# Four load buffers in the last stage of a convolution and mixture-of-experts kernel, and another order of its first loads

## What is computed

```python
def _branch(x, w, d):
    f = lax.conv_general_dilated(x, w, (1, 1), [(d, d), (d, d)], rhs_dilation=(d, d), ...)
    f = jax.nn.softmax(f.reshape(N, g, K, H * W), axis=2)
    out = jnp.einsum('ngrkp,ngkp->ngrp', patches, f)
...
y = lax.conv_general_dilated(cat, w_proj, (1, 1), ...) + b_proj
x = x + relu(_group_norm(y, gn_gamma, gn_beta))
t = _to_tokens(x)                      # (2 * 9216, 256)
for e in range(8):
    h = gelu(tokens @ w1[e] + b1[e], approximate=False)
    out = out + combine[:, e:e+1] * (h @ w2[e] + b2[e])    # tokens = layer norm of t
x = _from_tokens(t + out)
```

## Time and profile before

| | us |
|---|---|
| median of 3 runs | 2598.38 |
| lowest and highest of them | 2595.76, 2602.71 |
| the profiled execution, in all | 2577.68 |
| its span, from the first to the last instruction | 2575.9 |
| last stage in that span, from the first load to the end | 2342.6 to 2575.9 |
| busy in the span: PE, DVE, ACT, POOL | 1997.6, 1636.2, 1257.9, 1087.0 |

### The profile page before, as it was taken

How to read it: one execution, slowest core, us unless ns; L and a number is a source line. 1 busy time by engine, 2 the same in 40 slices (tenths; PEclk the granted TensorE clock), 3 DMA queues, 4 the chain that set the end, 5 groups by cost and what they waited for, 6 DMA issues and landing times.

```text
span 2575.9 us, 60532 instructions
## 1 busy us (share of the span) xinstructions
PE 1997.6 (78%) x20124; PEld 1892.3 (73%) x20125; DVE 1636.2 (64%) x4385; ACT 1257.9 (49%) x2705; POOL 1087.0 (42%) x1444
## 2 busy tenths in 40 slices
PE   5898999999799798787877836451999999993332
PEld 5897999999799697777777725451999999993222
DVE  4576666665677576465555546454877888885554
ACT  4575443333477454444444434341777777771111
POOL 3566223222376413444344405675555566562000
PEclk9999999999799798788887955555999999996555
DMA  5332555665433366557566486544666555555887
GB/s 136 98 99 64 168 152 140 174 170 146 122 105 93 93 191 176 164 171 211 172 202 177 141 286 204 200 162 131 193 202 195 151 155 154 153 151 195 270 303 266
DMA packets 334947, 433.65 MB, mean 168 GB/s; under 512 B 87469, under 2 KB 260141, under 8 KB 333805
## 3 DMA queue, kind: packets, MB, share of 16 engines
q1 hardware_dynamic: 260945, 294.85, 39.6%
q0 software_dynamic: 41024, 97.10, 10.8%
q10 hardware_dynamic: 32784, 39.07, 4.6%
HBM read 277.12 MB, written 159.94 MB: 170 GB/s over the span
## 4 chain that ended last, share of the span: by engine, by line
PE 47%; DMA 13%; issue 13%; DVE 7%; ACT 6%; another core or an unknown queue 4%; POOL 4%; SPq 3%; DVEq 2%; POOLq 0%; ACTq 0%
PE ps_y L418 15%; PE ps_a L418 7%; PE ps_o L1022 6%; PE ps L418 5%; PE ps_b L959 4%; DMA expert_out<-e_out,dest 4%; DMA o_y<-expert_out 3%; DMA o_acc<-res_scratch 3%; POOL taps L2174 2%; POOL expert_out L2264 2%; PE ps_r L1135 1%; PE ps_tok L856 1%; DMA e_x<-expert_in 1%; PE ps_a L900 1%
## 5 line engine op out<-in xcount | busy, mean ns | idle before, releaser
L418 PE MATMUL ps_y<-cat_hi,wp 128*128 128x288 f32 x2048 | 496.2, 317 | 13.3 <-issue 9.6
L2220 POOL DMA_DIRECT2D patches<-rows_scratch x348 | 194.8, 599 | 594.9 <-PE ps_o L1009 398.5
L2264 POOL DMA_INDIRECT expert_out<-e_out,dest x304 | 316.9, 1042 | 237.7 <-issue 121.0
L418 PEld LDWEIGHTS ps_y<-cat_hi,wp 128*128 128x128 f32 x2048 | 363.7, 199 | 19.1 <-issue 18.0
L2174 POOL TENSOR_TENSOR taps<-taps,g_rows 96x108 f32<-96x108 f32 (+3 forms) x440 | 252.4, 600 | 168.6 <-ACT g_rows L1270 164.7
L418 PE MATMUL ps_y<-cat_lo,wp 128*128 128x288 f32 x1024 | 313.6, 306 | 7.1 <-issue 7.1
L1696 DVE SCALAR_TENSOR_TENSOR cat_lo<-ps_o,cat_hi 128x288 fp32r<-128x288 f32 (+1 forms) x576 | 228.4, 421 | 134.2 <-ACT cat_hi L1349 84.4
L1343 ACT ACTIVATE bands<-ps_b 112x288 f16<-112x288 f32 (+4 forms) x256 | 105.2, 411 | 401.7 <-PE ps_b L959 324.8
L1349 ACT ACTIVATE cat_hi<-ps_o 128x288 fp32r<-128x288 f32 (+1 forms) x576 | 213.3, 384 | 136.6 <-remote 73.5
L1688 DVE SCALAR_TENSOR_TENSOR bands<-ps_b,bands 112x288 f16<-112x288 f32 (+4 forms) x256 | 116.9, 457 | 250.5 <-ACT bands L1343 216.7
L418 PE MATMUL ps<-e_hi,w_now 128*128 128x256 f32 x1216 | 242.9, 283 | 0.4 <-issue 0.4
(11 more groups left out here) (242 smaller groups left out, 4961.1 us busy)
## 6 DMA issues: line engine op xcount, KB each, us to landing
e_x<-expert_in SPq DMA_DIRECT2D x152, 260.0 KB
o_y<-expert_out SPq DMA_DIRECT2D x48, 768.0 KB, 5.7
patches<-rows_scratch SPq DMA_DIRECT2D x160, 192.0 KB
patches<-rows_scratch SPq DMA_DIRECT2D x256, 108.0 KB
patches<-rows_scratch SPq DMA_DIRECT2D x192, 112.0 KB
x_in<-in_x SPq DMA_DIRECT2D x48, 384.0 KB, 3.7
rows_scratch<-rows_st SPq DMA_DIRECT2D x48, 384.0 KB, 4.3
y_scratch<-y_acc SPq DMA_DIRECT2D x48, 384.0 KB
```

The costliest lines, as they stand in the source:

```text
L418: mm = eng.matmul(out, lhs[p], rhs[q], start=start and n == 0, stop=stop and n == 2)
L2220: pool.dma_start(patch_target(s, n), patch_source(m, s, n)).then_inc(patch_pooled[s % RING], 16)
L2264: pool.indirect_dma_start(out=ys_dram, out_offset=bass.IndirectOffsetOnAxis(ap=at, axis=0), in_=e_out[:, u, j], in_offset=None).then_inc(e ...
```

## The change

It has three parts.

1. **Last stage.** `o_y`, `o_acc` and the semaphores `o_loaded` become four (`OB = 4`); `o_sum`, `ps_t` and `o_out` stay two. The four `o_` tensors are now allocated where `w1` and `w2`, the experts' weights, lie, which are dead by then. All loops of the stage run over four groups instead of two.
2. **Start.** SyncE issues `ident`, the first two `x_in`, `wg_stage` and one bias before the barrier, with semaphores of their own; nine constants follow one by one in its iterations 3 to 11. The splits of `wg` and `wp_own` come behind the first normalisation, that of `wp` behind step 0. ScalarE's first `keep_own` waits for all three splits, since `y_acc` lies over `wp_stage`.
3. **`sel` and the codes** are issued by ScalarE, after its steps 4 and 10, instead of by SyncE in iteration 6.

```diff
+OB = 4
+        with ExitStack() as r1:
+            o_y = sbuf(r1, "o_y", [128, OB, TT, TOP, C])
+            o_acc = sbuf(r1, "o_acc", [128, OB, TT, C])
+            o_sum = sbuf(r1, "o_sum", [128, 2, TT, C])
+            o_out = sbuf(r1, "o_out", [128, 2, CC, TC])
         w1 = sbuf(ctx, "w1", [128, E, 2, CC * C], F32R)
...
-        N_CONST = 12
+        N_CONST = 9
...
+            sp.dma_start(ident[:], a["k_ident"]).then_inc(ident_in, 16)
+            for k in range(2):
+                sp.dma_start(x_in[:, k], x_dram[0, :, :, k * T:(k + 1) * T]).then_inc(x_loaded[k], 16)
+            sp.dma_start(wg_stage[:], a["w_gen"]).then_inc(first_in, 16)
+            sp.dma_start(gn_par[:, 0], a["b_proj"]).then_inc(bias_in, 16)
...
-                    if k == 6 and m == 0:
-                        sp.dma_start(sel[:], a["k_sel"]).then_inc(c_consts_in, 16)
-                        sp.dma_start(filt_t[2 * FCOL:KF], a["k_codes"]).then_inc(c_consts_in, 16)
+                    if m == 0 and 3 <= k < 3 + len(later):
+                        dst, src = later[k - 3]
+                        sp.dma_start(dst, src).then_inc(consts_in, 16)
...
             def load_outputs(t, residual):
-                for u in range(2):
+                for u in range(OB):
...
-                    wait(sp, o_summed, t * 2 + (u + 1))
+                    wait(sp, o_summed, t * OB + (u + 1))
...
-            pe.wait_ge(consts_in, 16 * N_CONST)
+            pe.wait_ge(ident_in, 16)
...
+                    if m == 0 and k == 0:
+                        pe.wait_ge(w_lo_done, 1)
                     tap_products(k, 0)
...
+                    if m == 0 and k == 0 and o == 0:
+                        act.wait_ge(bias_in, 16)
+                        act.wait_ge(w_lo_done, 3)
                     n = unit_at["own", m, k, o]
...
+                    if m == 0 and k == 0:
+                        weights_hi(2)
+                    if m == 0 and k == 4:
+                        act.dma_start(sel[:], a["k_sel"]).then_inc(c_consts_in, 16)
+                    if m == 0 and k == 10:
+                        act.dma_start(filt_t[2 * FCOL:KF], a["k_codes"]).then_inc(c_consts_in, 16)
...
-                        wait(act, o_stored[u], t * 16 + m * (16 * CPAIRS))
+                        wait(act, o_stored[u], t * (8 * OB) + (m * (16 * CPAIRS) + n // 2 * 16))
...
-                wait(dve, o_turned, t * 2 + (u + 1))
+                wait(dve, o_turned, t * OB + (n + 1))
```

More of the change, by code:

```diff
@@ L313, in build @@
                 dest = sbuf(r2, "dest", [128, 2, S // 128], I32)
-            with ExitStack() as r2:
-                o_y = sbuf(r2, "o_y", [128, 2, TT, TOP, C])
-                o_acc = sbuf(r2, "o_acc", [128, 2, TT, C])
-                o_sum = sbuf(r2, "o_sum", [128, 2, TT, C])
-                o_out = sbuf(r2, "o_out", [128, 2, CC, TC])
         with ExitStack() as r1:
@@ L840, in _ @@
                 if m:
+                    pe.wait_ge(consts_in, 16 * N_CONST)
                     group_sums(0, ps_a)
@@ L908, in turn_filters @@
                     pe.wait_ge(f_split, m * BATCHES + b + 1)
+                    if m == 0 and b == 0 and h == 0:
+                        pe.wait_ge(consts_in, 16 * N_CONST)
                     for r in range(R2 // 2):
@@ L1217, in _ @@
             enter(pe, 7 * N_ENG)
-            with pe.Fori(0, PAIRS) as t:
-                for u in range(2):
-                    wait(pe, o_summed, t * 2 + (u + 3))
-                    wait(pe, o_copied, t * 2 + (u + 1))
+            with pe.Fori(0, 2 * PAIRS // OB) as t:
+                for n in range(OB):
+                    u = n % 2
+                    wait(pe, o_summed, t * OB + (n + OB + 1))
+                    wait(pe, o_copied, t * OB + (n + 1))
                     for k in range(TT):
@@ L1672, in _ @@
                 factors(0)
+                if m == 0:
+                    weights_lo(0)
+                    weights_lo(1)
                 for k in range(GROUPS):
                     step(k)
+                    if m == 0 and k == 0:
+                        weights_lo(2)
                 weights(BATCHES - 3)
@@ L2137, in _ @@
             dve.wait_ge(res_loaded, 16 * EARLY)
-            with dve.Fori(0, EARLY // 2) as t:
-                for u in range(2):
-                    combine(t, u, True)
-            with dve.Fori(EARLY // 2, PAIRS) as t:
-                for u in range(2):
-                    combine(t, u, False)
+            with dve.Fori(0, EARLY // OB) as t:
+                for n in range(OB):
+                    combine(t, n, True)
+            with dve.Fori(EARLY // OB, 2 * PAIRS // OB) as t:
+                for n in range(OB):
+                    combine(t, n, False)
         @block.gpsimd
```

88 lines of the change are left out of this document (47 added, 41 removed).

## The result

| | kernel before | changed kernel |
|---|---|---|
| median | 2598.31 us (4 runs, 2595.76 to 2602.71) | 2536.02 us (4 runs, 2531.61 to 2541.81) |
| profiled execution, in all | 2577.68 us | 2541.81 us |
| its span | 2575.9 us | 2540.0 us |
| ratio | | 0.976, 95% interval 0.974 to 0.978 |

The kernel is 62.3 us faster by the medians. The forecast was 2553 us, 45 us faster.

A forecast was written before the change was run, and what follows sets the result against it. No engine bounds the last stage; its two load buffers set the pace. Gains of 41 + 2.5 + 2 = 45.5 us give 2532 profiled, plus 20.7 offset 2553 us; own range 2545 to 2566, 8-in-10 range 2534 to 2574.

The forecast's parts named there:

- full rate: Last stage: rival that the never-dry queue reaches 377 GB/s or more; stage 54 us shorter, 2540 us; 17 in 100.
- I take 350: Last stage: DMA rate of 350 GB/s assumed with loads always queued, giving 192.5 us against 233.3, 41 less.
- the late 4.5 us: Last stage, late groups, with an `o_acc` load: about 4.5 us per group forecast with four load buffers.
- The early 3.4: Last stage, early groups, without an `o_acc` load: about 3.4 us per group forecast with four load buffers.
- a pace by stores of 3.2 us: Last stage, early groups: pace if stores set it, (1.1 + 3.0 + 2.3)/2 = 3.2 us, below 3.4, so later stores cost nothing.
- The sign that the text had named for a wrong forecast: Last stage: the forecast is wrong if ScalarE's copies wait for stores, or if DMA share stays under 0.9.
- both of its terms: Start: statistics 4.5 us earlier; moved `wp` split delays TensorE about 1.9 us in step 1; net 2.5 us.
- A wait of 12.4 us: First convolution stage: VectorE's wait for a row store, 12.4 us instead of 14.5, so 2 us gained.
- order of issue over both queues: DMA engines: what SyncE issues later waits for transfers issued before it on ScalarE's queue, and the reverse; no sharing.
- The row it was drawn from: Last stage, old profile: store issued at 2498.15 us after a load pair landed after 7.5 us, at 2505.65.
- The rival with even sharing: First convolution stage: queues share evenly, so the `sel` stall would be gone; 10 us more, 2543 us; 15 in 100.
- The offset: Whole kernel: median 20.7 us above the profiled execution (2598.4 against 2577.7), carried over unchanged from 2532 to 2553 us.

The follow-up runs named there:

- -54.4 alone: The kernel before with only the last stage's four load buffers added, its start as before: 2337.12 us against 2394.07, ratio 0.976.
- the one on chip 14: The kernel before, unchanged, profiled a second time, on another chip: 2387.75 us profiled, 2394.07 us the median of seven runs.

## Why the prediction was right, and where it was not

The forecast of 2553 us was 17 us too high; the range of 2534 to 2574 holds 2536 at its low end. So the forecast's own range of 2545 to 2566, with 45 in 100, missed. The case that came is the rival "full rate" (2540), given 17 in 100. The parts of the sum:

| term | forecast | measured |
|---|---|---|
| part 1, last stage | -41 | -55.5 in the profiles, -54.4 alone |
| part 2, start | -2.5 | -3.9 |
| part 3, `sel` | -2 | -4.7 |
| sum | -45.5 | -64.1 |
| medians | 2598.4 to 2553 | 2598.3 to 2536.0 |

**Part 1: right mechanism, rate too small.** The term that failed is "I take 350". It came from dividing GB/s by the share in the stage itself, 332 and 344, as if that quotient stayed as it was once loads are queued. In the late part it is 386 now (405 at 1.05), and with four `o_out` buffers 382 early and 387 late. Weighted over the first two parts the changed kernel moves 378 GB/s; with it the prediction's own sum (63.7 MB, 2.4 us ahead, 8.1 us behind) gives 179.0 us for the 177.8 measured. The row with many loads queued, 377 GB/s at 1503 us, was in hand and was put at the end of the range, because its stage moves larger pieces. It was the nearer one; that a queue which doesn't run dry is what made it so is argued, no run varied the size of the pieces. Per group, the late 4.5 us came out as 3.87. The early 3.4 came out as 3.42, and that is luck: it was worked out from 350 GB/s, and it was the stores that made it. The first seven early groups took 2.42 us each, VectorE's own pace, as long as no buffer had to be waited for.

**Stores: named, priced, and dismissed by a margin that wasn't there.** The prediction computed a pace by stores of 3.2 us early and found it below 3.4 from the bytes. The first number was near (3.42 measured). The second was 2.94 (the pace with four `o_out` buffers), so stores did pace the early part. This cost 8.5 to 10 us, hidden in the total because the rate was under-estimated by more. The sign that the text had named for a wrong forecast, ScalarE's copies waiting for stores, did appear, with 120.5 us; the wait told where the loop was held, but its size said little of what it cost.

**Part 2** was under-estimated in both of its terms: the statistics came 5.3 us earlier (4.5 expected), and the split of `wp` took back 1.4 us (1.9 expected).

**Part 3: a good number from a reading that fell.** A wait of 12.4 us was forecast and 11.4 came, but the reason given (order of issue over both queues) does not hold, and the number is luck: stores overtake loads, `x_in` landed before `sel` was through, and cutting `sel` into four parts halves the landing of the row store (10.2 us for 20.5). What holds a transfer up is one packet of the other queue for each of its own, and up to the end of the row store that came to nearly all of `sel`, as by order of issue it would have been all. The row it was drawn from, a store that landed after 7.5 us behind two loads, fits both readings; it does not tell them apart, and nothing in the text had asked for one that does. The rival with even sharing rested on the Trainium skill ("DMA: Bandwidth & Descriptors", queues, rings and completion order), which says that an engine goes round robin between queues packet by packet. The traces agree, with 11 and 10 packets and with 45 and 46 in the two stretches above. What failed in that rival is the price: I gave the row store half of 26 GB/s, and half of the packets is a tenth of the bytes when the other side's are 9216 B and one's own 1024. The gain of 4.7 us beats the 2 forecast because a step of 8.68 us that followed the stall (97.23 to 105.91) is gone too, and the stalled step itself is 3.3 us shorter (16.5 for 19.75), where only 2 were counted.

**The offset.** 20.7 us were carried over from profile to median, and this held in effect: the stages' 64.1 us off the median of before give 2534.2, and 2536.0 was measured. But the offset is no constant of the kernel. The profile of after lies 5.8 us above its median, the one on chip 14 6.3 us below.

## What to carry over

Give a loop that is bound by transfers more buffers at both ends: four for loads gained 55 us, and four for stores 8.5 to 10 more, but only once the loads were queued; take the DMA rate for the estimate from the stretch of the profile in which the queue never runs dry, not from the stage's own GB/s divided by its share. Look for transfers whose number of rows has a small largest divisor up to 16: splitting 94 rows into 80 and 14 took the wait of 11 us for the row store away and gained 8.9 us, where moving the transfer to ScalarE's queue had left most of the wait. Price the traffic of another queue by packets: long rows beside short ones take most of an engine's time. And before a result is put down to a change, look at the stretches that it doesn't touch: here they differed by 28 us between two profiles of one kind of chip and by 190 us between chips.

## What the runs showed of the hardware that I had not expected

- Of four numbered chips, one takes 2593.5 us for the kernel before and three take 2394 to 2395. By the profile of before and the one on chip 14, 174 of the 188 us between the middles lie between the second image's first patches and the first load of the experts' stage, and 13 in the experts' stage; the first image and the last stage agree within 4 us.
- The queues of SyncE and ScalarE take turns on a DMA engine packet by packet (10 and 11 in 2 us, 46 and 45 in 3 us), with packets of 9216 B against 1 KB and with 2304 B against 1 KB. Beside packets of 9216 B a row store of 1 KB packets took 20.5 us to land, beside packets of 2304 B 10.2, and 3.6 with `sel` not yet issued (at 60.67 us).
- An issue can block its engine: 5.96 us for a small load behind `sel` on SyncE's queue (1.03 in the changed kernel), 6.95 us for the last quarter of `sel` on ScalarE's, where the first took 0.52.
- The busy share of the DMA engines isn't how much of their rate is used: 355 GB/s at 1.00, 405 at 1.06.
- A transfer of 94 rows goes over two engines from ScalarE's queue, and over many more from GpSimd's (846 KB landed in 6.2 us, at a share of 0.44 for that queue).
